# Routing weights of a feed-forward layer spread over partitions by broadcast loads from a scratch array, not by matmuls

## What is computed

```python
x = x + attention(layernorm(x))
xf = layernorm(x)
yg = xf @ shared_gw.T                       # shared expert, 352 hidden units
y, g = split(yg, 2);  shared = (silu(g) * y) @ shared_dw.T
scores = sigmoid(xf @ gate_w.T)             # 8 experts
topk_idx = top_k(scores + gate_bias, 2)
w = scores[topk_idx] / sum(scores[topk_idx])
for e in range(8):                          # 176 hidden units each
    we = sum(where(topk_idx == e, w, 0))
    g_e, u_e = split(xf @ up_w[e].T, 2)
    out += ((silu(g_e) * u_e) @ down_w[e].T) * we[:, None]
x = x + shared + out
```

## Time and profile before

| | us |
|---|---|
| median of 3 runs | 3279.95 |
| lowest and highest run | 3260.17, 3297.73 |
| span of the profiled execution | 3278.4 |
| feed-forward: first step of the last chain (L1671) | 2884.21 |
| tile 0, first block on the chain | 2906.32 |
| tile 1, 2, 3, first block | 3003.61, 3093.79, 3185.66 |
| last addition into y (DVE) | 3274.61 |

### The profile page before, as it was taken

One profiled execution on the slowest core, in us unless ns is written; L12 is line 12 of the kernel. 1 busy time (PEld: TensorE's weight loads), 2 busy tenths in 40 slices (PEclk: granted clock), 3 DMA queues, 4 the chain that ended last, 5 costly groups with the idle time before them and its releaser, 6 DMA issues. The chain is left out here.

```text
span 3278.4 us, 48421 instructions
## 1 busy us (share of the span) xinstructions
PE 2940.9 (90%) x14232; PEld 2043.1 (62%) x14232; DVE 2404.1 (73%) x4837; ACT 1621.8 (49%) x3516; POOL 1308.9 (40%) x1577
## 2 busy tenths in 40 slices
PE   7999999688889898898988989898898888879999
PEld 3555555466667666676666766677676667635554
DVE  6777777678887888878888788878888888632322
ACT  6666666445555555555555555545555555311110
POOL 3667677534344434344343443333444334300000
PEclk9999999889999999999999999999999999989999
DMA  3556556622122221232222322222322222030000
GB/s 135 228 214 239 231 204 239 185 46 39 39 53 55 50 44 39 43 65 51 43 40 41 66 50 43 39 41 48 59 54 39 41 40 41 15 107 20 7 7 7
DMA packets 443033, 249.60 MB, mean 76 GB/s; under 512 B 401488, under 2 KB 413488, under 8 KB 440624
## 3 DMA queue, kind: packets, MB, share of 16 engines
q1 hardware_dynamic: 442816, 246.90, 27.7%
HBM read 141.88 MB, written 104.99 MB: 75 GB/s over the span
## 5 line engine op out<-in xcount | busy, mean ns | idle before, releaser
L265 DVE SCALAR_TENSOR_TENSOR A_acc<-A_psY,A_w,A_acc 128x410 f32<-128x410 f32 (+1 forms) x720 | 419.2, 637 | 151.6 <-ACT A_acc L334 151.6
L832 POOL TENSOR_TENSOR B_WT<-B_WT,B_G 128x128 f32<-128x128 f32 (+2 forms) x224 | 190.9, 852 | 779.1 <-issue 448.1
L1136 ACT ACTIVATE B_WL<-B_psT 128x128 f32<-128x128 f32 (+2 forms) x480 | 150.3, 313 | 530.2 <-PE B_psT L1555 530.2
L405 PE MATMUL A_psY<-A_xT,A_w 128*128 128x413 f32 (+1 forms) x960 | 347.2, 510 | 9.1 <-PE A_psAG L411 7.7
L192 POOL TENSOR_TENSOR A_outs<-A_outs,A_acc 128x410 f32<-128x410 f32 (+1 forms) x240 | 229.7, 987 | 216.8 <-ACT A_outs L342 216.8
L405 PEld LDWEIGHTS A_psY<-A_xT,A_w 128*128 128x128 f32 x960 | 180.2, 189 | 165.5 <-issue 164.2
L1047 DVE TENSOR_TENSOR B_NC<-B_NC,B_psM 128x256 f32<-128x256 f32 x480 | 199.0, 414 | 114.8 <-PE B_psM L1582 95.7
L1050 DVE TENSOR_REDUCE B_W<-B_NC 128x64 f32<-128x320 f32 x512 | 248.7, 486 | 17.6
L1582 PE MATMUL B_psM<-B_BD,B_WL 128*128 128x128 f32 x1536 | 238.7, 297 | 9.2
L334 ACT ACTIVATE A_acc<-A_psY,A_w 128x410 f32<-128x410 f32 (+1 forms) x240 | 166.1, 692 | 162.9 <-PE A_psY L405 161.2
L1582 PEld LDWEIGHTS B_psM<-B_BD,B_WL 128*128 128x128 f32 x1536 | 197.2, 198 | 75.5 <-ACT B_WL L1136 74.7
(11 more groups left out here) (198 smaller groups left out, 7045.7 us busy)
## 6 DMA issues: line engine op xcount, KB each, us to landing
B_KQ<-scr SPq DMA_DIRECT2D x96, 512.0 KB, 6.6
scr<-A_outs SPq DMA_DIRECT2D x48, 615.0 KB, 3.5
scr<-A_outag SPq DMA_DIRECT2D x32, 615.0 KB, 5.2
scr<-A_outs SPq DMA_DIRECT2D x48, 409.0 KB, 2.5
A_xc<-nbeta SPq DMA_DIRECT2D x16, 1024.0 KB, 6.1
B_A<-scr SPq DMA_DIRECT2D x32, 512.0 KB, 4.9
B_C<-scr SPq DMA_DIRECT2D x32, 512.0 KB, 4.5
B_G<-scr SPq DMA_DIRECT2D x32, 512.0 KB, 4.6
```

Source lines behind the costliest of these rows:

```text
L265: nc.vector.scalar_tensor_tensor(a, y, w[:, s, col:col + 1], a, ALU.mult, ALU.add)\
L405: last = nc.tensor.matmul(psY[p][:, y0:y0 + HALO + t1 - t0], wp[:, p, kt, :], xT[:, kt, t0:t1 + HALO], start=kt == 0, stop=kt == KT - 1)
L832: tt(dst, dst, gr, ALU.mult).then_inc(wsc.sem, 1)
L1136: copy = lambda out, in_: nc.scalar.activation(out, in_, ACT.Copy)
```

## The change

The spread matrix, its matmuls, their waits and the PSUM buffers psW are gone. There is a scratch array `route` in device memory, 8 experts by 2048 tokens, and wB in SBUF, two buffers of [128, 11, 512], which holds for each hidden row of each block the weight of its expert. Once ACT has copied a tile's weights, SP stores the 8 rows of wT to the scratch array, waits for the landing, and loads each expert's row of 512 tokens into all partitions that need it by a broadcast: one DMA for each stretch of rows of one expert in one block (`expert_rows`). DVE waits for all of a tile's loads before its first weighting. In tile 0 the weightings come two at a time from block 8 on, in the other tiles one in each block from 3 on as before. PE's weight transposes of tile 0 stand before block 2.

```diff
+def expert_rows(m):
+    out, row = [], 128 * m
+    while row < min(128 * (m + 1), E * HE):
+        e = row // HE
+        end = min(128 * (m + 1), HE * (e + 1))
+        out.append((e, row - 128 * m, end - 128 * m))
+        row = end
+    return out
...
-        spread = sb("spread", [E, E * HE])
...
+        wB = sb("wB", [128, 2, ET, TF])
+        route_d = nc.dram_tensor("route", (E, T), FP32).ap()
...
-        psW = [ctx.enter_context(nc.psum_tensor(f"C_psW{i}", [128, 512], FP32)) for i in range(2)]
...
-        wb = Count(sem("spread_ps"), ET)
+        NROWS = sum(len(expert_rows(m)) for m in range(ET))
+        rst = Count(sem("route_st"), 1, 16)
+        wbl = [Count(sem(f"weights_spread{s}"), NROWS, 16) for s in range(2)]
...
             load(0, 1, TF)
+            def spread(i):
+                wait(sp, wm, i, 1)
+                sp.dma_start(route_d[:, TF * i:TF * (i + 1)], wT[:, i % 2, :]).then_inc(rst.sem, 16)
+                wait(sp, rst, i, 1)
+                if i >= 2:
+                    wait(sp, hw, i - 2, ET)
+                for m in range(ET):
+                    for e, r0, r1 in expert_rows(m):
+                        sp.dma_start(wB[r0:r1, i % 2, m, :], route_d[e, TF * i:TF * (i + 1)].partition_broadcast(r1 - r0))\
+                          .then_inc(wbl[i % 2].sem, 16)
+            spread(0)
             for i in range(NTF):
                 if i + 2 < NTF:
                     wait(sp, x1m, i, 1)
                     load(i // 2 + 1, i % 2, TF * (i + 2))
+                if i + 1 < NTF:
+                    spread(i + 1)
                 wait(sp, ym, i, NT)
...
+            def weighted(i, m):
+                wait(dve, wbl[i % 2], i // 2, NROWS)
+                wait(dve, hm, i, MT - ET + m + 1)
+                tt(hid[:, m, :], hid[:, m, :], wB[:, i % 2, m, :], ALU.mult).then_inc(hw.sem, 1)
...
-                    if m < ET:
-                        wait(dve, wb, i, m + 1)
-                        wait(dve, hm, i, k + 1)
-                        tt(hid[:, m, :], hid[:, m, :], psW[m % 2][:], ALU.mult).then_inc(hw.sem, 1)
+                    if k >= (8 if i == 0 else MT - ET):
+                        for _ in range(2):
+                            if done <= k - (MT - ET):
+                                weighted(i, done)
+                                done += 1
...
                 wait(act, wp, i, 1)
+                if i >= 2:
+                    wait(act, rst, i - 2, 1)
...
-                    if k == 3:
-                        if i == 0:
-                            weights(0)
-                        wait(pe, wm, i, 1)
-
+                    if k == 2 and i == 0:
+                        weights(0)
                     wait(pe, hm, i, k - 1)
...
-                    if m < ET:
-                        wait(pe, hw, i, m - 1)
-                        mm(psW[m % 2][:], spread[:, 128 * m:128 * (m + 1)], wT[:, i % 2, :], start=True, stop=True).then_inc(wb.sem, 1)
```

More of the change, by code:

```diff
@@ L1688, in _ @@
             wait(sp, st, NTF, 0)
+            wait(sp, rst, NTF, 0)
             for s in range(2):
                 wait(sp, x_ld[s], NTF // 2, 0)
+                wait(sp, wbl[s], NTF // 2, 0)
         @block.gpsimd
@@ L1694, in _ @@
             n = 0
-            for m, v in ((eps[:], EPS), (spread[:], 1.0)):
-                nc.gpsimd.memset(m, v).then_inc(const, 1)
-                n += 1
+            nc.gpsimd.memset(eps[:], EPS).then_inc(const, 1)
+            n += 1
             for e in range(E):
@@ L1700, in _ @@
                 n += 1
[L1701 to L1705, removed]
             pool.wait_ge(const, n)
-        NCONST = 2 + E + 2
+        NCONST = 1 + E
         @block.vector
@@ L1780, in route @@
                 assert n[0] == rt.per
+            def weighted(i, m):
+                wait(dve, wbl[i % 2], i // 2, NROWS)
+                wait(dve, hm, i, MT - ET + m + 1)
+                tt(hid[:, m, :], hid[:, m, :], wB[:, i % 2, m, :], ALU.mult).then_inc(hw.sem, 1)
             def tile(i):
+                done = 0
                 for k, m in enumerate(order):
```

## The result

The changed kernel took 3233.75 us (median of 4 runs, 3223.85 to 3251.01) beside 3283.43 us of the kernel before (4 runs, 3260.17 to 3297.73): a ratio of 0.986 with a 95% interval of 0.9823 to 0.9897. Forecast were 3237.7 us and 1.3% less. Measured once more later, with 6 runs beside 11 of the kernel before, it was 3237.99 against 3278.02 us, ratio 0.9882 (0.9852 to 0.9912).

What follows compares the result with a forecast made beforehand. PE was taken to bound the feed-forward stage. Terms: -47.9 (spreads) + 3.9 (normalisation) + 1.5 (routing, tile 0) + 0.3 (next routing) = -42.2 us, transfers zero, giving 3237.7 us, range 3216 to 3266.

Steps and rivals of the forecast that it cites:

- PE is the bound, and what a spread costs: Feed-forward stage: PE sets the pace; without spreads tiles 0 to 2 save 11.83 us each, tile 3 12.4.
- The normalisation: Before the transposes behind block 8, PE waits for xn: 1.8 us in tiles 1 and 2, 0.3 in tile 0.
- Routing of tile 0: Weight transposes now before block 2: PE waits for DVE's last routing step until 2917.66; cost 1.5 us.
- Routing of the next tile: Routing in block 10: no wait in tiles 1 and 2; waits of 0.3 us together in tile 0.
- The transfers: Store and 18 broadcast loads per tile take 20 to 24 us; cost zero, with 3 to 8 us cover in tile 0.
- Rival (b): Loads come one after another, 2.6 us each: 47 us lost together, kernel at 3285, no gain; chance 0.08, including a part.
- the harmless delay: Loads cost nothing if DVE waits only until 2950 in tile 0, or they land by E(13) + 43.4 us later.
- rival (d): Bigger gain: steps behind a spread give back 1.7 us, low-clock stretches (3 to 6 us) don't return: 3231; chance 0.07.
- the sum: All terms together: -42.2 us, giving 3237.7 us, 1.3% less; chance 0.66.
- Rival (a): Clock falls at PE's new waits (2.1 us tile 0, 1.8 us tiles 1 and 2): +10 us, 3248; chance 0.15.
- the forecast's sentence on 2.2 us of idling: Against rival (a): at tile 1's end, a 2.2 us gap was followed by a full-clock down projection of 24.43 us.

Runs made afterwards that it cites:

- the undone move: Changed kernel with PE's weight transposes of tile 0 put back before block 3: tile 0 takes 80.97 us, 2.42 less.
- loads in turn: Changed kernel with SP waiting for each of the 18 broadcast loads to land before issuing the next: four tiles take 372.6 us, 53.1 more.
- weighting from block 3: Changed kernel with tile 0's weightings one in each block from block 3, not from block 8: tile 0 takes 108.9 us, 25.5 more.
- last block last: Changed kernel with down projection sums in block order, PE waiting for the last block only ahead of it: tile 1 77.36 us, tile 3 72.3, 2.5 less each.

## Why the prediction was right, step by step

**PE is the bound, and what a spread costs.** Right. Tile 3 has none of the added costs and went from 88.93 to 74.76 us; 1.70 us of the difference is a low-clock stretch that the kernel before had in its last down projection (26.13 us) and this one not. The other 12.47 us stand against 12.4 forecast. The doubled spread shows the two parts of the price. The weighting takes 0.692 us from wB and took 0.687 us from psW, so its difference was rightly put at zero.

**The normalisation.** Right in place and size. The forecast had 8.57 us from E(6) to the end of xn; it is 3006.24 to 3014.83, 8.59 us, in the earlier trace rows's order of ACT and DVE. The wait is 1.8 us, and it was gone with one block more. In tile 0 it is 0.2 us instead of 0.3.

**Routing of tile 0.** Right: PE waits 2.1 us; 1.5 us net was forecast, and the undone move gave 2.4 us with its side effects. The 1.5 us counted against the kernel before, which had a wait for ACT there; the 2.1 us against the changed one.

**Routing of the next tile.** Forecast 0.3 us in tile 0; block 13 started at 2951.81 where PE was ready at about 2951.7: 0.1 us. Its gate half then takes 1.98 instead of 1.72 us, so the place costs 0.4 us in all. No wait in tiles 1 and 2.

**The transfers.** Right: forecast 20 to 24 us from the copy of the weights to the landing, measured 23.2 (2914.93 to 2938.17), so the slower of the two rows used (two loads of 512 KB in 7.5 us) was the nearer one. The issues take 13 us and not 9. The cover of tile 0 was all that kept this off the path: DVE waited 2.4 us and could have waited some 6: with the loads in turn 28.0 us of its wait became 21.3 us of PE's. Rival (b), the loads one after another, did not occur. When it was forced, its price of 2.6 us a piece was right (2.63), and its 47 us stand against stalls of 39.2 us and a stage longer by 53.1 us; it had the harmless delay too short and the clock behind the stalls not at all. The Trainium skill (page DMA: Bandwidth & Descriptors, section Bandwidth) asks for transfers of 1 MiB or more for three quarters of the peak, by figures for transfers issued from GpSimd; these are SP's. In direction the trace agrees: 132 GB/s in pieces of 32 to 256 KB, 172 GB/s for 1024 KB in 6.1 us. It decides nothing where the transfer is covered.

**What was left out.** Tiles 0 to 3 changed by -13.90, -10.33, -10.34 and -14.17 us, -48.7 in all, where -42.2 was forecast. Low-clock stretches make 5.3 us of the difference: the kernel before had 3.4 us in tile 0, 1.7 in tile 2, 1.7 in tile 3 and 2.3 in the first block, the kernel after 1.7 in tile 2 and 2.1 in the first block. That was one half of rival (d). What remains is 1.2 us; 0.8 of it are the gate scores (1.88 to 1.69 us) and the weight transposes (0.53 to 0.44 us), which were put at zero with 1.7 us as the other bound. So the stage came out where rival (d) put it, and not where the sum did: 3279.95 less 48.7 is 3231.2, (d) had 3231 at a chance of 0.07, and the sum had 3237.7. The medians, 3233.75 and later 3237.99, are too coarse to tell the two, and that the second lies 0.3 us from the forecast is luck. They moved by 49.7 us in the first measurement and by 40.0 us in the second. The changed kernel's stage was the same in both traces (319.5 and 319.7 us) while its start moved by 14 us, so most of that difference probably comes from the stages ahead.

Most of the low clock that went was more than a lucky draw. The 3.4 us of tile 0 and the 1.7 us of tile 2 stood in the middle of a tile, around block 10, with no wait of PE ahead of them. With the spread doubled the same place had low clock in tiles 0, 1 and 2. In the nine kernels without the spread, 27 such tiles, it never did. Why is open, since no run takes the spread away and nothing else, but the forecast left this out of its sum.

**The clock.** Rival (a) gave each new wait of about 2 us a low-clock stretch of 3.4 us. Behind the new waits (2.1 and 1.8 us) none is seen in this trace, nor in its repeat. In the experiments it is not so rare: seven kernels without the spread keep the 2.1 us wait in tile 0, and in three of them (loads in turn, weighting from block 3, last block last) the gate half behind it takes 3.1 to 3.4 us instead of 1.72. Behind 15 waits of 1.6 to 1.8 us at the transposes none does. So rival (a) holds for one of its three waits, in some executions, at half its price.

It was also argued from the gap at the end of one tile that such gaps do nothing, and that is too strong; nor was PE idle there for 2.2 us. The spread of block 13 ran in that gap, and PE idled 1.2 us each time, so the forecast's sentence on 2.2 us of idling rested on 1.2 us:

```profile
PE C_psX L1924 <- DVE C_hid L1786: 4.8, 4, 1.2
```

Nine kernels here keep the 2.2 us or more from the last block to the down projection. In seven of them, without the spread, PE idles through all of it (2.2 us), and 12 of 28 down projections take 26.0 to 26.1 us instead of 24.4; in the two with the spread (1.2 us idle before, 0.8 us with the spread doubled) 4 of 8 do. In the two kernels without the gap none of 8 does. The gap is followed by low clock in nearly half of the cases, at 1.7 us, and its length in idle time does not order them. The edit that took the gap away also changed the order of the projection's sums, and no run separates the two; why the low clock comes in one tile and not in the next is open.

## What to carry to other kernels

When an engine that sets the pace is relieved, look at which work of the next stage is tied to an event of its own and not to that engine's: it will be waited for by exactly its distance less the new, shorter one, and one block more of lead removes the wait. A transfer that replaces compute is free only up to the moment at which the waiting engine's other work in the same queue is needed; here that point was worked out in microseconds per piece, and the distance to it (2.6 us in turn against 1.2 when all are in flight) decided between 1.4% gained and nothing. Compare stage by stage: the spans of untouched stages moved by more than 10 us from run to run, while tiles 1 to 3 of the changed kernel repeated to 0.01 us.

## What the runs showed of the hardware that was not expected

A matmul whose weights have 8 rows costs 0.19 us at the change from weights of 128 rows and 0.19 us at the change back, beside its own 0.86 us (spread twice). Each of the five stalls of PE of 5.5 to 21.3 us was followed by a block partly or mostly at the lower level of 1.2 GHz (granted clock 0.54 over 7 us around the third stall of the loads in turn); the four of that run cost 2.4 to 3.2 us more than their length, the one of 18.7 us (weighting from block 3) 1.7 us more. And loads of 32 to 256 KB from one small array overlap well: 2.63 us each in turn, 21.8 us for 18 when all are issued at once.
